# Two fused attention layers on one core: the six middle batches as straight-line code instead of a loop

## The reference, cut to what matters

```
B, C, T = 8, 256, 1024                                # batches, channels, pixels
# layer 0: group norm (32 groups), then 8 heads of 32 channels
h   = (x - mean) * rsqrt(var + 1e-5) * gn_w + gn_b
q, k, v = split(qkv_w @ h + qkv_b)                    # per head, scaled by 32 ** -0.25
w   = softmax(q.T @ k)                                # 1024 x 1024 for each head
x   = x + proj_w @ (w @ v) + proj_b
# layer 1: one head with 32 channels for q and k, 256 for v
out = gamma * (Wv @ x) @ softmax((Wq @ x).T @ (Wk @ x)).T + x
```

## Time and profile before

| what | value |
|---|---|
| median of 3 runs | 1619.43 us (1619.39 to 1620.1) |
| the profiled execution: its time | 1615.41 us |
| the profiled execution: its span | 1613.5 us |
| mean granted TensorE clock | 0.954 |
| instructions in the span | 25511 |

### The profile page before, as it was taken

The page is one execution under the profiler, slowest core; times in us unless marked ns, Lnnn a source line. Parts: engine busy times, 40 slices in busy tenths (PEclk is TensorE's granted clock), DMA queues, the critical chain, the costliest instruction groups (busy, mean ns, idle before and its releaser), DMA issues.

```text
span 1613.5 us, 25511 instructions
## 1 busy us (share of the span) xinstructions
PE 1500.4 (93%) x7120; PEld 897.8 (56%) x7120; DVE 1132.3 (70%) x1916; ACT 752.1 (47%) x1377; POOL 1199.0 (74%) x560
## 2 busy tenths in 40 slices
PE   4889798999999999999999999999999999999968
PEld 1454354558545774558555674457555584556437
DVE  3776668877687677877688777877788777684243
ACT  2046354653546444653546445554546535563412
POOL 3069887895779777895889877796878958797804
PEclk9689889999999999999999999999999999999979
DMA  4040304030411214030220314020140304000100
GB/s 125 17 131 1 79 8 98 21 80 29 107 45 24 57 54 107 21 80 14 78 70 20 80 53 107 21 65 23 48 106 21 80 29 104 21 1 8 46 20 27
DMA packets 38741, 85.74 MB, mean 53 GB/s; under 512 B 10304, under 2 KB 20416, under 8 KB 38592
## 3 DMA queue, kind: packets, MB, share of 16 engines
q1 hardware_dynamic: 38208, 82.88, 20.5%
q0 software_dynamic: 384, 1.05, 0.3%
HBM read 18.29 MB, written 8.39 MB: 17 GB/s over the span
## 4 chain that ended last, share of the span: by engine, by line
PE 76%; DVE 9%; issue 7%; SPq 3%; ACT 2%; DMA 1%; POOL 1%; DVEq 0%; ACTq 0%; POOLq 0%
PE pv L516 14%; PE work L555 13%; PE st L485 13%; PE pv L494 11%; PE work L612 7%; DVE mpart L834 4%; PE work L575 4%; PE work L619 3%; PE work L587 3%; SPq L349 3%; PE work L581 2%; PE st L477 2%; PE work L561 2%; PE rec L533 1%; POOL acc L810 1%
## 5 line engine op out<-in xcount | busy, mean ns | idle before, releaser
L810 POOL TENSOR_TENSOR acc<-acc,probs 128x1024 f32<-128x1024 f32 x384 | 898.4, 2381 | 46.2 <-ACT probs L686 46.2
L686 ACT ACTIVATE probs<-st 128x512 f32<-128x512 f32 x1152 | 618.1, 602 | 480.0 <-PE st L485 375.4
L834 DVE TENSOR_REDUCE mpart<-work 128x1 f32<-128x512 f32 x1024 | 648.2, 681 | 184.2 <-PE work L555 180.8
L555 PE MATMUL work<-ks,qs 96*128 96x512 f32 x1024 | 428.2, 467 | 40.9 <-DVE vpd L880 14.5
L485 PE MATMUL st<-qs,ks 98*128 98x512 f32 x1024 | 404.4, 437 | 19.6 <-issue 17.2
L555 PEld LDWEIGHTS work<-ks,qs 96*128 96x128 f32 x1024 | 199.4, 198 | 203.0 <-DVE mpart L834 98.9
L810 POOL TENSOR_TENSOR acc<-probs 128x1024 f32<-128x1024 f32 x64 | 151.0, 2382 | 169.8 <-ACT probs L686 160.6
L485 PEld LDWEIGHTS st<-qs,ks 98*128 98x128 f32 x1024 | 197.4, 195 | 135.8 <-ACT probs L686 61.5
L494 PE MATMUL pv<-probs,vt 128*32 128x512 f32 x2048 | 252.5, 611 | 0.0
L516 PE MATMUL pv<-probs,l_vt 128*128 128x256 f32 x1024 | 235.7, 381 | 1.3 <-ACT raw L745 1.2
L516 PEld LDWEIGHTS pv<-probs,l_vt 128*128 128x128 f32 x1024 | 192.1, 190 | 35.6 <-ACT probs L686 5.0
(11 more groups left out here) (73 smaller groups left out, 967.3 us busy)
## 6 DMA issues: line engine op xcount, KB each, us to landing
qs<-part_hi SPq DMA_DIRECT2D x116, 128.0 KB, 2.6
ks<-part_hi SPq DMA_DIRECT2D x116, 128.0 KB, 2.4
xa<-in_x SPq DMA_DIRECT2D x16, 512.0 KB, 4.0
y<-in_x SPq DMA_DIRECT2D x8, 1024.0 KB, 5.4
out<-raw SPq DMA_DIRECT2D x32, 256.0 KB, 2.2
qs<-part_lo SPq DMA_DIRECT2D x60, 128.0 KB, 2.4
ks<-part_lo SPq DMA_DIRECT2D x60, 128.0 KB, 2.4
qs<-mrow SPq DMA_DIRECT2D x256, 2.0 KB
```

The costliest lines, as they stand in the source:

```text
L555: last = mm(bank, qs[g][0:HI_HI_LO, j, t0:t0 + P], ks[g][0:HI_HI_LO, j, half * HALF:(half + 1) * HALF], start=True, stop=True)
L686: nc.scalar.activation(probs[:, n % PRING, half * HALF:(half + 1) * HALF], st[:, (2 * n + half) % ST_BANKS, :], ACT.Exp).then_inc(s_exp1 i ...
L810: pool.tensor_tensor(a, first, probs[:, n % PRING, :], ALU.add).then_inc(s_add0, 1)
L834: last = dve.reduce_max(mpart[:, 4 * j + tb, half:half + 1], bank, AX.X)
```

## The change

On every engine, `run_steps` writes the six middle steps out one behind the other with `b` as a plain number, in place of one copy of the step in a loop. The order of the work on each engine, the plans, the buffers and what each wait asks for stay as they are.

```
             step("prologue", -1)
             step("first", 0)
-            with eng.Fori(1, B - 1) as b:
+            for b in range(1, B - 1):
                 step("steady", b)
             step("last", B - 1)
             step("epilogue", B)
```

## The result

The straight-line kernel takes 1608.85 us (median of 7 runs, 1608.11 to 1611.3) against 1619.39 us (7 runs, 1612.61 to 1620.1) in the same rounds: ratio 0.9944, 95% interval 0.9929 to 0.9959. It is 10.5 us faster. The forecast was no change, 1619.5 us, and its range ended at 1612.5 us.

The account below looks back on a forecast made before the run. TensorE, 93% busy, was taken to bound the kernel. Boundaries 1.2 us slower, 1 us taken back, other terms zero: 1615.4 + 0.2 profiled; at the median 1619.4 + 0.2, rounded to 1619.5 us, range 1612.5 to 1625 us.

Parts of the forecast that it names:

- Worth of the branch, 3.48 us each at its place: Loop's branch back, removed five times: TensorE's idle gap of 3.48 us goes where it stands, 17.2 us of issue waits.
- A wait at stop 17 takes its place: First matmul needing group 1's stack: would wait for the stack's DMA about seven times, 2.5 to 3 us each.
- The stack (not moved): SP's 24 stack copies at step boundaries: start no sooner, so 1.0 to 1.4 us of 3.48 us are left.
- The clock: Granted clock falls to 0.50 behind three-microsecond gaps, including stop 17's waits; priced in whole boundary stretches, 0.25 us more each.
- Rival B: Step boundaries: stack comes 1.26 us sooner without batch 7's copy stall; 8.8 us faster, 1610.6 us; chance 0.15.
- Five boundaries change: Sum over the five boundaries losing their branch: 5 x 0.25 = 1.2 us slower, 1 us taken back, 0.2 us left.
- From slot 11 on, a shift is carried through and no more: Rest of a step after slot 11: about 151.8 us whichever boundary came before, so no further change.
- The register instructions cost nothing: Instructions computing wait values on the engines' sequencers, removed: gain 0, with 1 us either way.
- Six times the code costs nothing: Longer straight-line code on each engine, read anew each step: no cost taken; sampled stretches slower by at most 0.3 us.
- Rival A: TensorE's branch gaps: all 17.2 us won, 1602.2 us; chance 0.07.

Follow-up runs that it names:

- the second profile of the same kernel: The straight-line kernel run again unchanged, in the rounds of the earlier-copies kernels: 1612.46 us, ratio 0.9966 against the loop kernel.
- the added waits: Straight-line kernel plus long-met TensorE waits: one before each bank fill of steady steps, 1611.07 us; or 234 per steady step, 1614.49 us.
- two and one branches: Loop kernel with two or three steps in the loop's body, register instructions kept: 1612.72 us with two branches back, 1609.79 us with one.
- reads inside against outside: Straight-line kernel plus 234 waits per steady step, TensorE's code reads outside the 24 copies: 1614.49 us; 110 more in batch 0, reads inside: 1629.46 us.

## Why the prediction was wrong

- *Worth of the branch, 3.48 us each at its place*: right. Without TensorE's branches the issue waits are gone (17.2 us over five), with TensorE's loop alone they are back (16.5 us).
- *A wait at stop 17 takes its place*: right, at all seven boundaries; it is part of why 17.2 us were not won.
- *The stack (not moved)*: this is the step that failed, in "the DMAs start no sooner". They start no sooner (2.14 us after the last score, 2.25 before with the registers), but they are through sooner. I took the two boundaries without a branch in the kernel before, 20.86 and 20.45 us to stop 17, as samples of the changed kernel. Both were bad samples: in the trace TensorE has a code read 9.0 us behind the first copy of batch 7, among the issues, and one 16.2 us behind the first of batch 1, while the last copies were landing. Three of seven boundaries of the changed kernel have none and are at 19.2 us. I saw the stall in batch 7's set of four and priced its absence at 1 us for all five boundaries; it is 1.3 us each, where it is absent. Behind each of the five branches TensorE reads code twice, 1.4 to 1.9 and 4.8 to 5.4 us after the last score, and the second read falls among the copies, but there the gap covers it.
- *The clock*: I let it fall behind each wait at stop 17. It fell behind two of seven. This is the second half of the same error: a wait that is 1.3 us shorter often keeps the clock, and that is worth as much again (29.92 against 32.67 us to slot 11). Two of the five that kept it are luck by the count at the end of this document: their waits were 2.45 and 2.35 us, with a read among the copies, and in the second profile of the same kernel the clock fell behind 2.45 and 2.32 us. Rival B had the size nearly right (1610.6 us) and the place, but left the clock where it was, and had a chance of 0.15.
- *Five boundaries change*: the sum left out the two without a branch. They changed too, by 4.5 and 1.9 us in the profiles. Into batch 1 a read no longer meets the copies and the clock stays up; into batch 7 one still does, and the clock stays up.
- *From slot 11 on, a shift is carried through and no more*: true but for the clock behind the second wait, which took back most of 7.2 us in the profiled run. The kernel before showed it already: I had read batches 1 and 6, at 151.8 us, while batches 2 and 5, where the clock fell, took 153.5 and 153.4 us.
- *The register instructions cost nothing*: right in size as far as the added waits stand for them, with a bound: 234 in 48 slots did cost about 1 us a step. What I left out is that without them a step is 1814 TensorE instructions in place of 2141, which moves the code reads. With them kept (two and one branches), no boundary that lost its branch was free of a read; without them, two of the five were.
- *Six times the code costs nothing*: right for TensorE's own stream. The Trainium skill says so too (page "Runtime: NRT & Kernel Launch", section "Instruction fetch mechanics"): crossing into the next block of code is mostly hidden. That holds for the engine that reads; such a read made SP's 24 copies 0.5 to 1.4 us longer (reads inside against outside), and this I had not priced.
- *Rival A*, the whole gain, fell in the plain kernel; with the copies started earlier it is passed: 1593.81 us is 24.9 us under the loop of the same rounds.

## What to carry to other kernels

A gap that is removed uncovers the chain behind it: find that chain's start and end before pricing the gap, and change both together (here 10.5 us for the loop alone, 24.9 us with the copies started earlier, 6.7 us for the earlier copies alone). When the kernel before shows the new state at one or two places, ask what else lies in those places; two samples that each held a disturbance, of 1.7 and 1.3 us at stop 17, hid a gain of 10.5 us. A semaphore count that stands for "all that came before" may wait for work that doesn't matter; the entry that the copy really needs was 1.6 us earlier.

## What the runs showed of the hardware

- A 16 KB read of TensorE's code among 128 KB copies holds up SP's queue: the longest time from one issue to the next is 0.9 to 2.2 us at 67 of the 68 boundaries with one read, in place of 0.64 us. Two kernels that differ in 110 waits long met, and so in where all these reads stand, are 15.0 us apart.
- The granted clock and a wait: over the fifteen profiles, it fell to 0.50 in or behind all 24 waits at stop 17 of 2.5 us and more, behind 14 of 21 of 1.8 to 2.5 us, behind 4 of 21 of 1.3 to 1.8 us, and behind none of 12 of 0.3 to 1.3 us. A fall for 3.41 us behind such a wait costs 1.4 to 1.6 us up to slot 11 (32.67 - 20.49 = 12.18 us from stop 17 to there, 29.92 - 19.18 = 10.74 us without it).
- The loop's time varies more than its three first runs showed: over 33 runs of the kernel before in one set of rounds, 1612 to 1628 us.
